# The preparation and the first attention of a two-layer transformer kernel, made one program

## The chip, the cores and the metric

One core of a Trainium2 chip runs the whole kernel as one launch. The time is device microseconds, the median of three runs. TensorE (PE) multiplies and transposes, ScalarE (ACT), VectorE (DVE) and GpSimd (POOL) work on tiles, SyncE (SP) issues the DMAs of this part. Each engine has a list of instructions in a fixed order, and waits on semaphores.

## The reference, cut to what matters

Six blocks follow each other, each added to the states `x` (4 batches of 128 tokens, width 512). The change touches the first alone, a cross attention of 16 heads of 64 over a context of 2048 rows per batch and the 128 states themselves:

```python
xn = layernorm(ctx_1024, ln_x_g, ln_x_b)                  # 4 x 2048 x 512
ln = layernorm(_layernorm(x), ln_l_g, ln_l_b)             # 4 x 128 x 512
q = ln @ Wq                                               # 4 x 128 x 1024
kv = concatenate([xn @ Wkv, ln @ Wkv], axis=1)            # 4 x 2176 x (1024 + 1024)
qn, kn = rmsnorm(q, qn_g) * 64 ** -0.5, rmsnorm(k, kn_g)  # per head of 64
attn = softmax(where(mask, qn @ kn.T, -max))
x = x + (attn @ v) @ Wout + bout
```

## The kernel before

Products that need more than bf16 are made of a high and a low bf16 part of each factor: three products hi x hi, hi x lo, lo x hi.

**`cross0_prepare` (L110 to L449)** is a stage of its own, with a barrier behind it. It loads states and the context of batch 0, normalises both (statistics on VectorE, the root on GpSimd), transposes them on TensorE in 128x128 tiles, splits the context into `x_hi` (ScalarE, L263) and `x_lo` (GpSimd, L229), splits the projection weights `Wkv` in four quads into `w_hi` and `w_lo`, and makes all queries: eight products in float32 (L442), norm, transposes, split, stores of `q_hi` and `q_lo` to DRAM.

**`cross0_attend` (L464 to L1190)** works in 16 units: unit u is batch u // 4, quad of heads u % 4. A unit has 17 steps, one for each 128 rows of keys (16 of context, the last the states). Step n of 272 has on TensorE, in this order:

- `project(n)`: twelve matmuls of 512 columns (L1074 to L1076) that give the keys and values of four heads for 128 rows; it waits for the values' low part of step n - 2
- `turn` (L1085): transposes of normalised keys, due three and four steps after the last projection e of a group of four (the fifth group of a unit is the states alone); `context` (L1093): transposes of the next batch's context. Both go into the one bank KT, and wait until its last user was read
- `values(n - 27)` (L1156 to L1158), `scores(n - 25)` (L1124, L1126), `maximum` (L1106), five to eight steps after e. In the first step of a unit's values they come after the maximum, and wait for `result()` of the unit before.

So LAG = 25 steps of projection run before the first scores. ScalarE copies each projection out (`copies`, L838 to L840), evacuates the turned keys, and does the exponentials. VectorE does in step n, in this order: `result`, `values_low`, `seed(n - 24)` (it writes minus the maximum into the score bank ahead of the scores of the next step, L959), `key_low`, `maximum` (L935), `key_norm` (L907), `key_sum` (L900), then normalising (L924) and statistics (L918, L919) of the next batch's context. GpSimd does in step n `key_root` (L780, L781), `context_root`, the low part of the exponentials (L816), mask blocks (L770) and the low part of the turned context. Tables written out by hand say in which step each of these stands: `key_sum` in step e, `key_root` and `key_norm` in e + 1, `turn` in e + 3 and e + 4. The second group of a unit has e at place 7 of the 17, so its root stands at place 8 and its turns at 10 and 11.

Of the kernel before, what the change touches and what calls it, by code (L numbers as in the profile page):

```python
# [16 lines left out]
B = 4  # L17
# [92 lines left out]
def cross0_prepare(nc, t, X, keep, sb, sem):  # L110
# [4 lines left out]
    x_hi, x_lo = keep["x_hi"], keep["x_lo"]  # L115
    q_hi = sb("c0_qhi", [P, PAIRS, TOK], BF16)
    q_lo = sb("c0_qlo", [P, PAIRS, TOK], BF16)
    L = sb("c0_l", [P, B, D], F32)
    xa = sb("c0_xa", [P, 4, D], F32)
    xb = sb("c0_xb", [P, 4, D], F32)  # L120
    LT = sb("c0_lt", [P, C, TOK], F32)
    lt_hi = sb("c0_lthi", [P, C, TOK], BF16)
    lt_lo = sb("c0_ltlo", [P, C, TOK], BF16)
    wq = sb("c0_wq", [P, C, INNER], F32)
    wst = sb("c0_wst", [P, 2, C, 512], F32)
    q32 = sb("c0_q32", [P, B, INNER], F32)
    sq = sb("c0_sq", [P, 2, 512], F32)
    xf = sb("c0_xf", [P, 2, 512], F32)
    ss = sb("c0_ss", [P, B, H0], F32)
    rn = sb("c0_rn", [P, B, H0], F32)  # L130
    gl = sb("c0_gl", [P, C], F32)
    bl = sb("c0_bl", [P, C], F32)
    gx = sb("c0_gx", [P, C], F32)
    bx = sb("c0_bx", [P, C], F32)
    gq = sb("c0_gq", [P, 1], F32)
    gk = sb("c0_gk", [P, 1], F32)
    gqk = sb("c0_gqk", [P, 1], F32)
    lst = sb("c0_lst", [P, B, 6], F32)
    lmv = sb("c0_lmv", [P, B, 2], F32)
    lsd = sb("c0_lsd", [P, 3, B], F32)  # L140
    st = sb("c0_st", [P, 4, 6], F32)
    mv = sb("c0_mv", [P, 4, 4, 2], F32)
    rstd = sb("c0_rstd", [P, 4, 4], F32)
    power = sb("c0_power", [P, 4], F32)
    x_in, id_in, vec_in, gv_in, wq_in = sem("c0_x_in"), sem("c0_id_in"), sem("c0_vec_in"), sem("c0_gv_in"), sem("c0_wq_in")
    ctx_in, w_in = [sem(f"c0_ctx_in{j}") for j in range(4)], [sem("c0_w_in0"), sem("c0_w_in1")]
    w_hi_done, w_lo_done = sem("c0_w_hi"), [sem("c0_w_lo0"), sem("c0_w_lo1")]
    dve_step, pool_step, consts, power_ready = sem("c0_dve"), sem("c0_pool"), sem("c0_consts"), sem("c0_powr")
    var_ready, sd_ready, l_norm = sem("c0_var"), sem("c0_sd"), sem("c0_l_norm")
    l_tp, lt_done, lt_hi_done, lt_lo_done = sem("c0_l_tp"), sem("c0_lt"), sem("c0_lt_hi"), sem("c0_lt_lo")  # L150
    stat_done, xroot_done, xn_ready = sem("c0_stat"), sem("c0_xroot"), sem("c0_xn_r")
    ln_tp, ln_evac, xhi_done, xlo_done = sem("c0_ln_tp"), sem("c0_ln_ev"), sem("c0_xhi_d"), sem("c0_xlo_d")
    q_mm, q_sq, q_ss = sem("c0_q_mm"), sem("c0_q_sq"), sem("c0_q_ss")
    ms_ready, qsd_ready, qn_done, g_ready = sem("c0_ms"), sem("c0_qsd"), sem("c0_qn"), sem("c0_gr")
    q_tp, q_hi_done, q_lo_done = sem("c0_q_tp"), sem("c0_q_hi"), sem("c0_q_lo")
    lt_out, q_out = sem("c0_lt_out"), sem("c0_q_out")
    QN = INNER // 512
    XT = 4 * C

    def ctx(j):  # L160

        return (X, xa, xb, X)[j]

    def turned_q(b, half):

        return ps[:, 2 + half, :].rearrange("p (r n) -> p r n", n=P)

    with nc.Block() as block:

        @block.sync  # L170
        def _(sp):
            def context(j):
                sp.dma_start(ctx(j)[:], t["ctx"][0, j * 512:(j + 1) * 512, :].rearrange("(i p) d -> p i d", p=P))\
                  .then_inc(ctx_in[j], 16)

            def weights(g):
                wkv = t["L0_xattn_Wkv"].rearrange("(c p) n -> p c n", p=P)
                for half in range(2):
                    sp.dma_start(wst[:, g % 2, :, half * 256:half * 256 + 256],
                                 wkv[:, :, half * INNER + g * 256:half * INNER + g * 256 + 256])\  # L180
                      .then_inc(w_in[g % 2], 16)

            sp.dma_start(L[:], t["x"].rearrange("b p d -> p b d")).then_inc(x_in, 16)
            sp.dma_start(identf[:], t["eye"]).then_inc(id_in, 16)
            for dst, src in ((gl, "L0_xattn_ln_l_g_col"), (bl, "L0_xattn_ln_l_b_col"),
                             (gx, "L0_xattn_ln_x_g_col"), (bx, "L0_xattn_ln_x_b_col")):
                sp.dma_start(dst[:], t[src]).then_inc(vec_in, 16)
            context(0)
            sp.dma_start(wq[:], t["L0_xattn_Wq"].rearrange("(c p) n -> p c n", p=P)).then_inc(wq_in, 16)
            context(1)  # L190
            weights(0)
            for dst, src in ((gq, t["L0_xattn_qn_g"]), (gk, t["L0_xattn_kn_g"])):
                for h in range(2):
                    sp.dma_start(dst[h * DH0:h * DH0 + DH0, :], src.rearrange("(d a) -> d a", a=1))\
                      .then_inc(gv_in, 16)
            context(2)
            weights(1)
            sp.wait_ge(ln_tp, C)
            context(3)
            for g in range(2, QUADS):  # L200
                sp.wait_ge(w_lo_done[g % 2], 1)
                weights(g)
            sp.wait_ge(lt_lo_done, C)
            sp.wait_ge(lt_hi_done, C)
            for b in range(B):
                sp.dma_start(t["lt_hi_d"][b], lt_hi[:, :, b * P:(b + 1) * P]).then_inc(lt_out, 16)
                sp.dma_start(t["lt_lo_d"][b], lt_lo[:, :, b * P:(b + 1) * P]).then_inc(lt_out, 16)
            for b in range(B):
                sp.wait_ge(q_hi_done, 2 * b + 2)
                sp.dma_start(t["q_hi_d"][b], q_hi[:, :, b * P:(b + 1) * P]).then_inc(q_out, 16)  # L210
                sp.wait_ge(q_lo_done, 2 * b + 2)
                sp.dma_start(t["q_lo_d"][b], q_lo[:, :, b * P:(b + 1) * P]).then_inc(q_out, 16)
            sp.wait_ge(lt_out, 2 * B * 16)
            sp.wait_ge(q_out, 2 * B * 16)

        @block.gpsimd
        def _(pool):
            step = Steps(pool, pool_step)

            def root(j):  # L220
                pool.wait_ge(stat_done, j + 1)
                step(pool.tensor_scalar(rstd[:, j, :], mv[:, j, :, 1], 1e-5, None, ALU.add))
                pool.tensor_tensor(rstd[:, j, :], rstd[:, j, :], power[:], ALU.pow).then_inc(xroot_done, 1)

            def low(x):
                j, c = divmod(x, C)
                pool.wait_ge(xhi_done, x + 1)
                cols = slice(j * 512, (j + 1) * 512)
                pool.tensor_tensor(x_lo[:, c, cols], xf[:, x % 2, :], x_hi[:, c, cols], ALU.subtract).then_inc(xlo_done, 1)  # L229

            def weight_low(g):
                pool.wait_ge(w_hi_done, g + 1)
                pool.tensor_tensor(w_lo[:, :, g, :], wst[:, g % 2], w_hi[:, :, g, :], ALU.subtract)\
                    .then_inc(w_lo_done[g % 2], 1)

            pool.memset(power[:], -0.5).then_inc(power_ready, 1)
            pool.wait_ge(power_ready, 1)
            root(0)
            root(1)
            low(0)  # L240
            low(1)
            weight_low(0)
            for k in range(7):
                if k == 2:
                    root(2)
                if k == 4:
                    root(3)
                low(2 * k + 2)
                low(2 * k + 3)
                if k == 5:  # L250
                    weight_low(2)

        @block.scalar
        def _(act):
            def context(x):
                j, c = divmod(x, C)
                act.wait_ge(ln_tp, x + 1)
                if x >= 2:
                    act.wait_ge(xlo_done, x - 1)
                act.activation(xf[:, x % 2, :], ps[:, x % 2, :], ACT.Identity, bias=bx[:, c:c + 1],  # L260
                               scale=gx[:, c:c + 1]).then_inc(ln_evac, 1)
                act.wait_ge(ln_evac, x + 1)
                act.activation(x_hi[:, c, j * 512:(j + 1) * 512], xf[:, x % 2, :], ACT.Copy).then_inc(xhi_done, 1)  # L263

# [19 lines left out]
            for k in range(B * QN):  # L284
                act.wait_ge(q_mm, k + 1)
                if k >= 2:
                    act.wait_ge(q_ss, k - 1)
# [163 lines left out]

# [2661 lines left out]
```

## Time and profile before

| | us |
|---|---|
| median of three runs | 2538.76 (2532.03 to 2540.55) |
| profiled execution | 2541.76 |
| its span, first to last instruction | 2539.8 |
| `cross0_prepare`, to the first projection | 95.8 |
| first projection to the scores' first step | 79.3 |

In the profile PE is TensorE's matmuls, PEld its weight loads; a row of a timeline has the start in us, the duration in us, the engine, the line, the operation, the tiles and how many instructions were merged. A matmul's duration in a row is longer than the distance to the next one, since matmuls are pipelined: distances of starts are what it costs.

### The profile page before, as it was taken

How to read it: one execution, taken by the hardware profiler on the slowest of the kernel's cores; microseconds unless marked ns; L12 is line 12 of the kernel's file. 1: busy time of each engine (PE TensorE's matmuls, PEld its weight loads, DVE VectorE, ACT ScalarE, POOL GpSimd, SP SyncE). 2: the span in 40 equal slices, each digit the busy share in tenths (PEclk: the TensorE clock that was granted, in tenths of full speed). 3: DMA queues.
4: the chain of work that ended last, by engine and by line, in shares of the span. 5: the costliest groups of instructions: out<-in, count | busy, mean ns of one | idle time of the engine just before them, and what ended most of it. 6: DMA issues, size and time to landing. Idle time of an engine off the chain costs nothing. (4 is left out here: it accounts for less than half of the span.)

```text
span 2539.8 us, 57508 instructions
## 1 busy us (share of the span) xinstructions
PE 2312.9 (91%) x21955; PEld 1499.9 (59%) x21955; DVE 1826.2 (72%) x3370; ACT 1557.3 (61%) x2912; POOL 1123.5 (44%) x895
## 2 busy tenths in 40 slices
PE   5799999999999999998888699995799899998795
PEld 3346656666566655666445577772567676776442
DVE  7478877888788867776363699995777777766236
ACT  4347666666666666665234499883377676887313
POOL 4437666666666665554100000004367676656100
PEclk8899999999999999998899799997999999999897
DMA  6223233224222321124321699984533434224002
GB/s 212 52 71 93 84 106 83 75 75 125 82 70 79 107 72 42 42 60 152 113 104 39 219 368 364 365 301 165 163 110 118 127 121 127 88 89 161 30 1 85
DMA packets 256273, 313.56 MB, mean 123 GB/s; under 512 B 71792, under 2 KB 183024, under 8 KB 255104
## 3 DMA queue, kind: packets, MB, share of 16 engines
q1 hardware_dynamic: 252048, 301.76, 37.1%
q10 hardware_dynamic: 3312, 6.03, 0.6%
q8 instruction: 175, 2.87, 0.5%
q0 software_dynamic: 640, 2.10, 0.3%
q14 instruction: 98, 0.80, 0.1%
HBM read 226.23 MB, written 47.91 MB: 108 GB/s over the span
## 5 line engine op out<-in xcount | busy, mean ns | idle before, releaser
L816 POOL TENSOR_TENSOR a_plo<-a_p,a_phi 128x512 bf16<-128x512 f32 x272 | 316.0, 1162 | 358.9 <-ACT a_phi L870 358.1
L1074 PE MATMUL ps<-w,a_xhi 128*128 128x512 bf16 x1088 | 413.9, 380 | 6.0 <-PEq L3010 6.0
L1075 PE MATMUL ps<-w,a_xhi 128*128 128x512 bf16 x1088 | 413.8, 380 | 0.0
L1076 PE MATMUL ps<-w,a_xlo 128*128 128x512 bf16 x1088 | 413.8, 380 | 0.0
L2234 POOL TENSOR_TENSOR a_plo<-a_p,a_phi 128x512 bf16<-128x512 f32 x256 | 306.6, 1198 | 178.8 <-ACT a_phi L2271 169.7
L838 ACT ACTIVATE a_kraw<-ps 128x256 f32<-128x256 f32 x272 | 104.2, 383 | 373.5 <-PE ps L1076 371.8
L2366 DVE CUSTOM_DVE_ANT_0 a_junk<-ps,a_biasrow 128x512 bf16<-128x512 f32 x256 | 176.2, 688 | 117.6 <-PE ps L2506 114.6
L893 DVE TENSOR_TENSOR a_v<-ps,a_v 128x256 bf16<-128x256 f32 x272 | 114.3, 420 | 164.3 <-ACT a_v L840 162.8
L2266 ACT ACTIVATE a_p<-ps,a_mcol 128x512 f32<-128x512 f32 x256 | 174.8, 683 | 87.6 <-PE ps L2524 79.9
L907 DVE SCALAR_TENSOR_TENSOR a_kraw<-a_kraw,a_rn 128x1024 f32<-128x1024 f32 (+1 forms) x80 | 154.2, 1928 | 78.3 <-POOL a_rn L781 78.3
L781 POOL TENSOR_TENSOR a_rn<-a_rn,a_power 128x16 f32<-128x16 f32 (+1 forms) x80 | 204.0, 2550 | 6.6
L866 ACT ACTIVATE a_p<-ps,a_mcol 128x512 f32<-128x512 f32 x256 | 178.8, 699 | 21.7 <-POOL a_plo L816 12.7
L959 DVE CAST ps<-a_less 128x512 f32<-128x512 bf16 x256 | 174.6, 683 | 12.7 <-ACT a_p L866 12.6
L1076 PEld LDWEIGHTS ps<-w,a_xlo 128*128 128x128 bf16 x1088 | 106.6, 98 | 129.1 <-issue 1.3
L1075 PEld LDWEIGHTS ps<-w,a_xhi 128*128 128x128 bf16 x1088 | 106.6, 98 | 124.9 <-issue 1.1
L2489 PE MATMUL ps<-a_whi,c_hi 128*128 128x128 bf16 x1024 | 178.9, 220 | 1.4
L2489 PE MATMUL ps<-a_wlo,c_hi 128*128 128x128 bf16 x1024 | 178.7, 220 | 0.0
L2489 PE MATMUL ps<-a_whi,a_clo 128*128 128x128 bf16 x1024 | 178.6, 220 | 0.0
L870 ACT ACTIVATE a_phi<-a_p 128x512 bf16<-128x512 f32 x272 | 171.3, 630 | 8.7
L935 DVE CUSTOM_DVE_ANT_0 a_junk<-ps,a_mrow 128x512 bf16<-128x512 f32 x256 | 173.9, 679 | 0.0
L1074 PEld LDWEIGHTS ps<-w,a_xhi 128*128 128x128 bf16 x1088 | 106.6, 98 | 105.3 <-issue 7.4
L2271 ACT ACTIVATE a_phi<-a_p 128x512 bf16<-128x512 f32 x256 | 161.2, 630 | 8.1
(461 smaller groups left out, 6890.6 us busy)
## 6 DMA issues: line engine op xcount, KB each, us to landing
e_wst<-in_L_ffn_W SPq DMA_DIRECT2D x46, 2048.0 KB, 10.3
a_ks<-a_khi SPq DMA_DIRECT2D x256, 64.0 KB, 2.0
a_ks<-a_klo SPq DMA_DIRECT2D x256, 64.0 KB, 2.1
a_ct<-in_ctxT SPq DMA_DIRECT2D x16, 1024.0 KB, 6.3
a_ks<-k1h_d SPq DMA_DIRECT2D x128, 128.0 KB, 2.5
xa<-in_ctx SPq DMA_DIRECT2D x8, 1024.0 KB, 5.6
k1h_d<-a_khi SPq DMA_DIRECT2D x64, 128.0 KB, 2.1
k1l_d<-a_klo SPq DMA_DIRECT2D x64, 128.0 KB, 1.7
```

Of the source, the lines that this page charges most:

```text
L781: pool.tensor_tensor(rn[:, key_part(j)], rn[:, key_part(j)], power[:, key_part(j)], ALU.pow)\
L816: pool.tensor_tensor(p_lo[:, m % 3, :], p32[:, m % 2, :], p_hi[:, m % 3, :], ALU.subtract)\
L866: act.activation(p32[:, m % 2, :], ps[:, m % 2, :], ACT.Exp, **bias).then_inc(exp_done, 1)
L935: dve.tensor_tensor_reduce(junk[:], ps[:, bank_m(x), :], mrow[:, j * 512:(j + 1) * 512], 1.0, -3e38, ALU.add, ALU.max, mx[:, h, j:j + 1]). ...
L959: dve.tensor_copy(ps[:, m % 2, :], less[:]).then_inc(seeded, 1)
L1074: pe.matmul(out, x_hi[:, c, tile], w_hi[:, c, g, :], start=(c == 0), stop=False)
L1075: pe.matmul(out, x_hi[:, c, tile], w_lo[:, c, g, :], start=False, stop=False)
L1076: last = pe.matmul(out, x_lo[:, c, tile], w_hi[:, c, g, :], start=False, stop=(c == C - 1))
L2234: pool.tensor_tensor(p_lo[:, m % 3, :], p32[:, m % 2, :], p_hi[:, m % 3, :], ALU.subtract)\
L2266: act.activation(p32[:, m % 2, :], ps[:, m % 2, :], ACT.Exp, bias=mcol[:, u // 4, s:s + 1])\
L2366: dve.tensor_tensor_reduce(junk[:], ps[:, bank_m(x), :], biasrow[:, u // 4 % 2, j * 512:(j + 1) * 512], 1.0, -3e38, ALU.add, ALU.max, mx[: ...
L2489: last = pe.matmul(ps[:, VP, i * P:(i + 1) * P], x[:, b % 2, c, tile], w[:, 1, c, quad], start=(c == 0 and k == 0), stop=(c == C - 1 and k ...
```

## The change

`cross0_prepare` goes away and `cross0` does its work inside the attention's own steps. The first context block is loaded first, normalised, turned and split ahead of the loop; the first projection follows. Blocks 1 to 3, the states, the weights of quads 1 to 3 and the mask are prepared in steps 0 to 18. The queries are no longer made all at once in float32: `query_product` makes those of one unit from high and low parts, twelve matmuls of 256 columns in bank KT, one unit ahead; their norm goes with the last key group of a unit (`size` is 2 instead of 1), so they are squared, rooted, normalised, turned and split as keys are, and go from SBUF into `q_both` and `q_low`. The query weights (512 KB a unit) are loaded and split unit by unit. The second context tile `xn1` is gone, so context blocks are loaded later, and their statistics, normalising and turns stand in other steps.

```diff
-    def query_norm / query_high / query_low ...     (all of cross0_prepare)
...
+    WQ_LOAD, WQ_SPLIT, Q_MADE = (10, 6), (12, 8), (14, 12)
+    def size(u, j):
+        return 4 if j < 4 else 2 if u < UNITS - 1 else 1
...
-                ln_stat[at + ((9, 10, 13, 13) if late else (1, 2, 5, 5))[i]].append((b, j, i))
-                ln_norm[at + ((18, 21, 21, 22) if late else (10, 13, 13, 14))[i]].append((b, j, i))
-                ln_turn[at + ((25, 26, 29, 30) if late else (16, 17, 21, 22))[i]].append((b, j, i))
+            begin = at + ((10, 9, 6, 5)[j] if b == 1 else 5)
+                ln_stat[begin + (2, 3, 3, 4)[i]].append((b, j, i))
+                ln_norm[begin + (5, 5, 6, 6)[i]].append((b, j, i))
+                ln_turn[at + (((17, 21, 22, 25), (16, 17, 21, 22))[j] if b == 1 and j < 2 else (13, 16, 17, 21))[i]]\
+                    .append((b, j, i))
+            ln_load[begin].append((b, j))
...
+    def unit_at(n, place):
+        u, s = divmod(n, NT0)
+        return u if s == place[u > 1] and u < UNITS - 1 else None
...
         def _(sp):
+            head_load(0)
+            sp.dma_start(L, t["x"].rearrange("b p d -> p b d")).then_inc(l_in, 16)
+            ...
+            weights(0)
+            head_load(1)
+            query_weights(0)
...
+                u = unit_at(n, WQ_LOAD)
+                if u is not None:
+                    query_weights(u + 1, n)
                 for u, j, pr in k_turn[n]:
                     stack(u, j, pr)
+                    if j == 4 and u < UNITS - 1:
+                        queries(u + 1, k_hi[:, x, 2 * P:4 * P], k_lo[:, x, 2 * P:4 * P])
...
         def _(pool):
+            def query_weight_low(u):
+                pool.wait_ge(wq_hi_done, u + 1)
+                pool.tensor_tensor(wq_lo[:], wqs if u else wq0, wq_hi[:], ALU.subtract).then_inc(wq_lo_done, 1)
...
             for n in range(LAST):
+                if n < 2:
+                    head_low(4 + 2 * n)
+                    head_low(5 + 2 * n)
+                ...
+                if n in (12, 18):
+                    weight_low(2 if n == 12 else 3)
+                u = unit_at(n, WQ_SPLIT)
+                if u is not None:
+                    query_weight_low(u + 1)
                 for u, j in k_norm[n]:
                     key_root(u, j)
...
         def _(act):
                 if 0 <= n < N:
                     copies(n)
+                if n in (0, 1, 4, 5, 8, 9):
+                    head_context_parts(x)
+                    head_context_parts(x + 1)
+                ...
+                u = unit_at(n, WQ_SPLIT)
+                if u is not None:
+                    query_weight_high(u + 1)
                 for u, j, pr in k_turn[n]:
                     turned(u, j, pr)
                 for b, j, c in ln_turn[n]:
-                    context(b, j, c)
+                    context(n, b, j, c)
+                u = unit_at(n, Q_MADE)
+                if u is not None:
+                    query_copies(u + 1)
...
         def _(dve):
+            head_stat(0)
+            (statistics of the states)
+            head_norm(0)
+            weight_high(0), then w_lo of quad 0
+            head_stat(1), normalising of the states, head_norm(1)
             for n in range(FIRST, LAST):
...
                     values_low(n)
+                if n in (1, 3):
+                    head_stat(2 if n == 1 else 3)
+                if n in (3, 6):
+                    head_norm(2 if n == 3 else 3)
+                if n == 5:
+                    dve.wait_ge(q0_root, 1)
+                    (norm of the first queries)
+                if n in (6, 11, 17):
+                    weight_high({6: 1, 11: 2, 17: 3}[n])
...
         def _(pe):
+            def query_product(u):
+                ...
+                for c in range(C):
+                    pe.matmul(out, hi[:, c, :], wq_hi[:, c, :], start=(c == 0), stop=False)
+                    pe.matmul(out, hi[:, c, :], wq_lo[:, c, :], start=False, stop=False)
+                    last = pe.matmul(out, lo[:, c, :], wq_hi[:, c, :], start=False, stop=(c == C - 1))
+                last.then_inc(q_mm, 1)
+            for x in range(C):
+                head_turn(x)
             for n in range(FIRST, LAST):
                 if 0 <= n < N:
                     project(n)
+                if n == 0:
+                    states_turn()
+                if n in (0, 1, 4, 5, 8, 9):
+                    head_turn(x)
+                    head_turn(x + 1)
+                if n == 3:
+                    query_product(0)
+                if n == 5:
+                    query_turn()
                 (turn, context)
+                u = unit_at(n, Q_MADE)
+                if u is not None:
+                    query_product(u + 1)
...
-                stage(cross0_prepare, X, keep)
-                stage(cross0_attend, X, keep)
+                stage(cross0, X, keep)
```

Lines in brackets and a few short forms stand for code that is told in words above.

## Rows read from the trace of the kernel before

**Rows 1.** Windows: span, busy us of PE, PEld, DVE, ACT, POOL; clock, DMA share, GB/s.

```profile
0.00:95.80 95.80, 52.09 (x176) 30.84 (x177) 64.66 (x108) 38.45 (x62) 38.98 (x32) 0.81 0.50 154
175.10:1180.00 1004.90, 988.25 (x9049) 609.54 (x9047) 792.90 (x1510) 663.54 (x1481) 627.55 (x485) 0.99 0.29 81
```

**Rows 2.** Timeline at the seam of the two stages.

```profile
91.38 0.51 SPq L212 DMA_DIRECT2D q_lo_d<-c_qlo  x1
95.81 0.59 PE L1074 MATMUL ps<-w,a_xhi 128*128 128x512 bf16 x1 [5.97 <-PEq L3010]
```

**Rows 3.** Groups of instructions of the first 95 us: busy us, mean ns, idle before.

```profile
L229 POOL TENSOR_TENSOR a_xlo<-c_xf,a_xhi 128x512 bf16<-128x512 f32 x16 | 23.9, 1511 | 17.7 <-ACT a_xhi L263 17.7
L260 ACT ACTIVATE c_xf<-ps,c_bx,c_gx 128x512 f32<-128x512 f32 x16 | 12.3, 768 | 6.7 <-POOL a_xlo L229 6.2 <-PE ps L413 0.6
```

**Rows 4.** Timeline of the prepare stage.

```profile
6.02 2.47 DVE L358 BATCH_NORM_STATS2 c_lst<-c_l 128x6 f32<-128x512 f32 x4 [5.03 <-DMA c_l<-in_x]
16.15 2.19 ACT L280 ACTIVATE c_lthi<-c_lt 128x512 bf16<-128x512 f32 x4
16.16 1.92 DVE L318 TENSOR_SCALAR xa<-xa,c_mv,c_rstd 128x512 f32<-128x512 f32 x4 [1.72 <-POOL c_rstd L223]
28.41 4.07 POOL L233 TENSOR_TENSOR w<-c_wst,w 128x2048 bf16<-128x2048 f32 x1 [2.87 <-DVE w L324]
34.79 3.13 DVE L327 TENSOR_TENSOR w<-c_wst,w 128x2048 bf16<-128x2048 f32 x1
```

**Rows 5.** Windows of TensorE alone: span, busy us, granted clock, DMA share, GB/s.

```profile
33.00:39.40 6.40, 1.75 (x9) 0.76 0.58 173
39.40:43.00 3.60, 3.54 (x11) 0.50 1.07 319
```

**Rows 6.** Timeline of TensorE, the projection of step 25.

```profile
175.08 0.38 PE L1074 MATMUL ps<-w,a_xhi 128*128 128x512 bf16 x1
```

**Rows 7.** Timeline of GpSimd, place 8 of unit 5.

```profile
451.41 0.25 POOL L780 TENSOR_SCALAR a_rn<-a_ms 128x16 f32<-128x16 f32 x1 [0.23 <-DVE a_ms L900]
451.74 2.93 POOL L781 TENSOR_TENSOR a_rn<-a_rn,a_power 128x16 f32<-128x16 f32 x1
```

**Rows 8.** Timeline of ScalarE, the last of place 8's copies.

```profile
451.99 0.40 ACT L840 ACTIVATE a_v<-ps 128x256 bf16<-128x256 f32 x1
```

**Rows 9.** Timeline of VectorE, places 5 to 10 of unit 5.

```profile
442.27 0.68 DVE L918 BATCH_NORM_STATS2 a_st<-a_xn 128x6 f32<-128x512 f32 x1
...
443.78 0.18 DVE L919 BATCH_NORM_AGGREGATE a_mv<-a_st 128x2 f32<-128x6 f32 x1
...
454.70 2.18 DVE L907 SCALAR_TENSOR_TENSOR a_kraw<-a_kraw,a_rn 128x1024 f32<-128x1024 f32 x1 [0.59 <-POOL a_rn L781]
...
457.14 0.68 DVE L959 CAST ps<-a_less 128x512 f32<-128x512 bf16 x1
...
458.55 0.42 DVE L968 TENSOR_TENSOR a_ao<-ps,a_rs 128x256 f32<-128x256 f32 x1
```

**Rows 10.** Timeline of TensorE, place 10 of unit 5 and the next projection.

```profile
458.40 0.60 PE L1085 MATMUL ps<-identf,a_kraw 128*128 128x128 f32 x4
458.84 0.22 PE L1124 MATMUL ps<-a_qboth,a_ks 128*128 128x128 bf16 x1
...
459.50 0.19 PE L1156 MATMUL ps<-a_v,a_phi 128*128 128x65 bf16 x1
...
459.87 0.38 PE L1074 MATMUL ps<-w,a_xhi 128*128 128x512 bf16 x1
...
462.46 0.60 PE L1085 MATMUL ps<-identf,a_kraw 128*128 128x128 f32 x4
```

**Rows 11.** Timelines of GpSimd, VectorE and TensorE, places 7 to 10 of unit 4.

```profile
382.06 1.93 POOL L770 TENSOR_SCALAR a_mrow<-a_mrow 128x512 bf16<-128x512 uint8 x1
387.37 2.17 DVE L907 SCALAR_TENSOR_TENSOR a_kraw<-a_kraw,a_rn 128x1024 f32<-128x1024 f32 x1 [1.53 <-POOL a_rn L781]
390.14 0.60 PE L1085 MATMUL ps<-identf,a_kraw 128*128 128x128 f32 x4
```

More of the change, by code:

```diff
@@ L126, in cross0_prepare @@
[L126 to L147, printed above, removed]
@@ L600, in cross0_attend @@
             held_by = ("ln", part(*use) + 1)
-    def xn(n):
-        return (X, xn1)[n % 2]
+        if unit_at(n, Q_MADE) is not None:
+            before_q[unit_at(n, Q_MADE) + 1] = held_by
+            held_by = ("query", unit_at(n, Q_MADE) + 2)
     def bank_p(n):
@@ L870, in exponent @@
                 act.activation(p_hi[:, m % 3, :], p32[:, m % 2, :], ACT.Copy).then_inc(phi_done, 1)
-            act.wait_ge(vec_in, 48)
+            act.wait_ge(vec_in, 64)
+            for x in range(C):
+                head_context_parts(x)
+            query_weight_high(0)
             for n in range(FIRST, LAST):
@@ L987, in add_result, with head_stat @@
                 dve.tensor_tensor(X[:, b, :], X[:, b, :], ps[:, bank_o(b), :], ALU.add).then_inc(res_done, 1)
+            def head_stat(j):
+                dve.wait_ge(c_in[j], 16)
+                for i in range(4):
+                    last = dve.bn_stats(st[:, i, :], head_context(j)[:, i, :])
+                step(last)
+                for i in range(4):
+                    last = dve.bn_aggr(hmv[:, j, i, :], st[:, i, :])
+                last.then_inc(c_stat, 1)
+                dve.wait_ge(c_stat, j + 1)
@@ new lines, in head_norm, with weight_high @@
+            def head_norm(j):
+                dve.wait_ge(c_root, j + 1)
+                for i in range(4):
+                    last = dve.tensor_scalar(head_context(j)[:, i, :], head_context(j)[:, i, :], hmv[:, j, i, 0:1],
+                                             hrstd[:, j, i:i + 1], ALU.subtract, ALU.mult)
+                last.then_inc(c_norm, 1)
+            def weight_high(g):
+                dve.wait_ge(w_in[g % 2], 32 * (g // 2 + 1))
+                dve.tensor_copy(w_hi[:, :, g, :], wst[g % 2]).then_inc(w_hi_done, 1)
@@ new lines, in _ @@
+            dve.memset(onesb[:], 1.0).then_inc(consts, 1)
+            head_stat(0)
+            dve.wait_ge(l_in, 16)
+            for b in range(B):
+                last = dve.bn_stats(st[:, b, :], L[:, b, :])
+            step(last)
+            for b in range(B):
+                last = dve.bn_aggr(lmv[:, b, :], st[:, b, :])
+            last.then_inc(l_stat, 1)
+            dve.wait_ge(l_stat, 1)
+            head_norm(0)
+            weight_high(0)
+            dve.wait_ge(w_hi_done, 1)
@@ L1058, in bank_free @@
                 kind, count = held
-                pe.wait_ge(ktlo_done if kind == "turn" else ln_evac, count)
+                pe.wait_ge({"turn": ktlo_done, "ln": ln_evac, "query": q_cp}[kind], count)
             def project(n):
```

672 lines of the change are left out of this document (323 added, 349 removed).

## The prediction

> **What bounds the kernel now.** I read the windows by stage first [rows 1]. Up to 95.8 us no engine is full: TensorE is busy 52 us, VectorE 65. This is the prepare stage. From 175.1 to 1180 us TensorE is busy 988 of 1005 us at full clock, the other engines 62 to 79%: the attention is bound by TensorE, so each microsecond of work or wait that is put on TensorE there is added to the time, and each one taken from the time before it is gained. The seam comes next [rows 2]: the last query store is issued at 91.4, the first projection starts at 95.8. Then the timelines of one step of the steady attention, which show how much room each helper engine leaves ahead of TensorE's next use [rows 7 to 10]; this is where I expect the change to be decided. Call a place in a unit of 17 steps s0 to s16.
>
> **Part 1, the head: gain.** Context block 0 is now the first transfer, and a first transfer of 1 MB is used at 6.02 [rows 4]. Its statistics take 2.9 (2.47 and the aggregates), those of the latents stand before the normalising and take as much, the normalising 1.92 [rows 4]: 13.8. Then four chunks go through ScalarE (0.77, and 0.55 for the high part) and GpSimd (1.5 as the mean of the stage) with two buffers [rows 3, 4], about 8.5: the last low part at 22.4. The first weights' parts on VectorE (3.13 for the low one [rows 4]) are done by then. So the first projection moves from 95.8 to about 22.4: 73.4 earlier.
>
> Not all of it lasts to step 25, where the scores begin (175.08 now [rows 6]). TensorE gets, between projections, 12 chunk transposes of 0.44 [rows 10] (5.3), the latents' 16 (1.8) and the first query product with its turn (1.5), some of it at half clock: about 10. And it waits, because VectorE and GpSimd now do the rest of the preparation inside the steps. I followed each engine's written order with the durations of rows 3, 4 and 7 to 10; the waits that end last are estimates:
> - steps 3 and 4: statistics of blocks 2 and 3 and the normalising of 2 stand ahead of the values' low part: 2.0 and 3.4.
> - step 5: the first query's norm stands on VectorE behind the key norm, which waits on GpSimd behind two low parts and the query's root; TensorE waits at query_turn: 7.4.
> - steps 7 and 8: key_low behind block 3's normalising and weight_high, then the key stacks on the DMA queue behind six query copies: 2.7 and 2.2.
> - step 14: weight_low(2), 4.07 [rows 4], and the split of the next query weights stand on GpSimd ahead of the key root: 5.6, and 4.0 more at the query product, which needs the bank that key_low frees.
> - step 17: the transposes of context (1,0) wait for its normalising: 5.2.
> These are 32.5. Waits like these cost clock too: between 33.0 and 39.4 TensorE was busy 1.75 of 6.4 us, and the next 3.6 us ran at 0.50 [rows 5]; I take 3 us for it. Gain: 73.4 - 10 - 32.5 - 3 = 28. Bounds: 48, if the 7.4, the 9.6 of step 14 and the clock cost nothing; 20, if VectorE and GpSimd hold each other up all through: the low part takes 1.51 as a mean of the stage [rows 3], a quarter of the 4.07 for four times the columns is 1.02 [rows 4].
>
> The Trainium skill (SBUF — State Buffer, section "SBUF: two separate sides") says that GpSimd and a VectorE instruction with two SBUF inputs exclude each other for the whole instruction. The rows agree: 1.51 us where both work, 1.02 where GpSimd works by itself [rows 3, 4]. By that rule the first projection would come up to 3.1 later, at 25.5, and the gain would be 25.
>
> **Part 2, work added on TensorE in the steady part.** Twelve projection matmuls of 512 columns take 2.60 (459.87 to 462.46 [rows 10]); the query product has twelve of 256 columns: 1.30, in units 1 to 15; unit 1's is in part 1, so 14 x 1.3 = 18.2. The last key group of a unit turns four tiles instead of two: 0.22 (half of 0.44 [rows 10]) x 15 = 3.2. Together 21.4, a certain cost, as nothing else on TensorE goes away. That ScalarE (1.1 for the split, 0.8 for two copies, 0.4) and VectorE (about 1) get more per unit costs nothing by its sum, since they are not full; what counts is where it stands in the order.
>
> **Part 3, the split of the query weights at s8.** At s8 (s12 for units 0 and 1) ScalarE does query_weight_high after the step's copies, GpSimd query_weight_low, and in GpSimd's list this stands ahead of key_root. At the same step the root of the second key group is due. Now: key root from 451.41 to 454.68 [rows 7], key norm on VectorE 454.70 to 456.88 [rows 9], turn on TensorE at 458.40 [rows 10]: 1.5 of room. That this room is all there is, is seen where a mask block stood before the same root in the step before: key norm done at 389.54, turn at 390.14 [rows 11]: 0.6 left, so the root was about 0.9 late and TensorE did not wait.
>
> After: copies end at 452.4 [rows 8]; the high part of 128x1024 is half of 2.19 for 128x2048 [rows 4]: 453.5; the low part is half of 4.07: 2.0 to 2.1, to 455.6; the root 3.27, to 458.9; the key norm 2.18, to 461.1. The turn is 2.7 late. Behind the key norm on VectorE are queued, in the ten units with context to normalise, two statistics that the new table puts at s8 (442.27 to 443.96 is such a pair: 1.7 [rows 9]), then the next values' low part and the seed that the scores of s10 need (1.0): 463.8 instead of a free start at 458.84: 5.0 late. Then at s10 the values wait for result(), which stands behind a maximum (0.7), another statistic (0.8) and its own 0.6: 465.95 against 459.50, 6.4 late [rows 9, 10]. The next projection starts 6.4 late; the steps after it find what they need, so it neither grows nor is won back. Without the statistics (units 12 to 14) the same chain gives 3.9. Unit 1, with s12 and a query product at s14 behind key_low: about 8. Sum: 10 x 6.4 + 3 x 3.9 + 8 = 84. Bounds: 38, if only the late turn costs (14 x 2.7); above, 14 more if the low part takes 3.0 instead of 2.05 (twice the 1.51 of rows 3), and the clock, below.
>
> The other moved pieces I cost at nothing: the context load at s5 and the 512 KB of query weights at s6 have more than two steps to land (a first megabyte is used at 6.02 [rows 4], a step is about 4), and stacks that queue behind them would wait inside the stall above; queries now go from SBUF, with as many transfers, five steps ahead of use.
>
> **Sum**, from the profiled execution, 2541.76 (span 2539.8; the three timed runs have a median of 2538.76, 3 less): 2541.8 - 28 + 21.4 + 84 = 2619, in terms of the median 2616.
>
> **Rivals.**
> - *The split is absorbed (faster).* Place: key_root at s8. If high and low part together delay the root by less than 1.5, no turn is late, nothing queues, and 2539 - 28 + 21 = 2532 is left (2512 with the head's upper bound). For it: GpSimd is busy 62% [rows 1]. Against it: the split can't start before the copies end at 452.4 [rows 8], a microsecond after the root starts now [rows 7], and 3.1 us of two instructions don't fit into 1.5. It decides at a delay of 1.5; I work out 4.2. Chance 0.15.
> - *The clock falls in the stalls (slower still).* In 458.4 to 466.3 TensorE would work some 1.5 of 7.9 us; a stretch of that kind (1.75 of 6.4) was followed by 3.6 us at 0.50 [rows 5], which costs half of it, 1.8. With 14 such places: 25 more, 2641. Against it: VectorE, not TensorE, would then be behind for a step, and hides part. The Trainium skill (TensorE: Matmul & The Clock Gate, section "HAM oscillation — how this bites in real kernels") tells of just this pattern, idle gaps that make each burst start at half rate; by it the time would be this rival's. Chance 0.17.
> - *The transfers decide.* 1.5 MB queued at s5 and s6 ahead of the first key stack of a unit makes the maximum at s8 late, and the split's input too, in the three units with a read-back: 3 to 10 us on top, about 2624. For it: TensorE waits for these stacks in program order. Against: such a wait falls into the stall, which is longer. Chance 0.08.
>
> **How the numbers follow.** The forecast as worked out has 0.60, its own range is 2550 (gain 48, stalls 38) to 2640. With the clock and transfer rivals the slower side holds 0.85, less 0.02 for sums of favourable bounds; the absorbed split has 0.15, of which 0.12 is faster by over 0.3% (about what a measurement of this kernel tells from no change) and the rest within it. The range 2530 to 2655 leaves out most of the faster case and the worst of the clock.
>
> **What would show it.** Right: first projection near 22 us, scores near 147; a unit of 17 steps that grows by 5 to 8 us; GpSimd's key root waiting behind query_weight_low; TensorE's waits led by the turn for the key norm and by the scores for the seed. Wrong: TensorE still busy over 97% in the steady part (the split absorbed), or a first projection after 30 us. The weakest points are the head's list of waits and that VectorE's order keeps the statistics behind the key norm.

## The result, and the profile after

The changed kernel takes 2654.85 us (median of four runs, 2650.73 to 2656.74), the kernel before beside it 2537.74: a ratio of 1.046, with a 95% interval of 1.0445 to 1.0474, 117 us slower. The forecast was 2616, 77 slower. The profiled execution has a span of 2654.3.

The head first. Timelines of TensorE in the changed kernel: its first projection, the waits that last longest, and the first projection of the step in which scores begin.

```profile
23.74 0.61 PE L1070 MATMUL ps<-w,a_xhi 128*128 128x512 bf16 x1 [3.49 <-POOL a_xlo L600]
...
62.35 0.69 PE L1194 MATMUL ps<-identf,a_p 128*128 128x128 f32 x2 [8.38 <-DVE a_p L979]
...
104.63 1.12 PE L1082 MATMUL ps<-identf,a_kraw 128*128 128x128 f32 x4 [4.50 <-DVE a_kraw L817]
108.94 0.37 PE L1186 MATMUL ps<-a_wqhi,a_lqhi 128*128 128x256 bf16 x1 [3.19 <-issue]
...
126.02 0.47 PE L1090 MATMUL ps<-identf,xa 128*128 128x128 f32 x1 [4.65 <-DVE xa L839]
...
152.68 0.38 PE L1070 MATMUL ps<-w,a_xhi 128*128 128x512 bf16 x1
```

The first projection has come from 95.8 [rows 2] to 23.7, 72 us earlier; the scores from 175.1 [rows 6] to 152.7, 22.4 earlier. The other 50 us went, on the way, into waits (31.8) and into work that now stands there, some of it at a lower clock.

Then the steady attention: a window of the changed kernel that holds units 1 to 14, from the end of place 7 of unit 1 (columns as in [rows 1]).

```profile
152.00:1240.00 1088.00, 990.95 (x8613) 606.41 (x8751) 761.05 (x1452) 661.91 (x1466) 630.74 (x471) 0.96 0.29 78
```

TensorE was busy 98% here [rows 1], now 91%, and the granted clock is 0.96 in place of 0.99. The table of waits over the same part (waiter, who released it: us in all, times, longest) says where TensorE stands and what is late before it; "issue" is a wait for which the profile names no engine.

```profile
DVE a_kraw L817 <- POOL a_rn L570: 127.1, 70, 4.8
...
POOL a_wqlo L608 <- ACT a_wqhi L722: 38.4, 14, 5.7
...
PEld ps L1103 <- issue: 23.1, 9, 5.0
...
PE ps L1070 <- issue: 19.7, 6, 5.2
PE ps L1082 <- DVE a_kraw L817: 18.5, 10, 2.7
...
PE ps L1153 <- issue: 14.0, 13, 1.7
PE ps L1121 <- DVE ps L874: 13.6, 11, 1.9
```

TensorE waits for the key norm (L1082), for the seed (L1121) and for the result that frees the values' bank (L1153), in 10 to 13 of 14 units each; the key norm waits for the root, and GpSimd sat idle until the query weights' high part came. The largest sum of TensorE's stands before these three: in units 3 to 11 the maximum at place 8 (its weight load, L1103; the wait shows again at the projection behind it, L1070) waits for the key stacks. Timelines of TensorE's weight loads and of its matmuls in unit 7:

```profile
636.96 0.10 PEld L1103 LDWEIGHTS ps<-a_ks,a_qboth 128*128 128x128 bf16 x1 [4.34 <-issue]
...
637.37 0.63 PE L1070 MATMUL ps<-w,a_xhi 128*128 128x512 bf16 x1 [4.57 <-issue]
```

The last stack that it needs was issued at 629.86 and landed 7.04 us later, at 636.90. Units 3 to 11 wait so for 0.7 to 5.0 us, and less at the turn two places on for it: not at all in 3, 7 and 11. One unit shows the order. Timelines of ScalarE, GpSimd, VectorE and TensorE at places 8 to 10 of unit 6, one engine after the other; the counterpart of [rows 7 to 10].

```profile
554.68 0.39 ACT L693 ACTIVATE a_v<-ps 128x256 bf16<-128x256 f32 x1
555.11 1.06 ACT L722 ACTIVATE a_wqhi<-a_xf 128x1024 bf16<-128x1024 f32 x1
...
556.25 2.13 POOL L608 TENSOR_TENSOR a_wqlo<-a_xf,a_wqhi 128x1024 bf16<-128x1024 f32 x1 [2.37 <-ACT a_wqhi L722]
...
558.34 0.25 POOL L569 TENSOR_SCALAR a_rn<-a_ms 128x16 f32<-128x16 f32 x1
558.68 2.93 POOL L570 TENSOR_TENSOR a_rn<-a_rn,a_power 128x16 f32<-128x16 f32 x1
561.57 1.15 POOL L665 TENSOR_TENSOR a_plo<-a_p,a_phi 128x512 bf16<-128x512 f32 x1
...
552.80 1.21 DVE L810 TENSOR_REDUCE a_ms<-a_sq 128x16 f32<-128x1024 f32 x1
...
561.64 2.17 DVE L817 SCALAR_TENSOR_TENSOR a_kraw<-a_kraw,a_rn 128x1024 f32<-128x1024 f32 x1 [4.43 <-POOL a_rn L570]
563.73 0.68 DVE L833 BATCH_NORM_STATS2 a_st<-xa 128x6 f32<-128x512 f32 x1
...
565.64 0.68 DVE L874 CAST ps<-a_less 128x512 f32<-128x512 bf16 x1
...
567.85 0.42 DVE L883 TENSOR_TENSOR a_ao<-ps,a_rs 128x256 f32<-128x256 f32 x1
...
563.86 0.66 PE L1082 MATMUL ps<-identf,a_kraw 128*128 128x128 f32 x4 [1.18 <-DVE a_kraw L817]
566.39 0.23 PE L1121 MATMUL ps<-a_qboth,a_ks 128*128 128x128 bf16 x1 [1.87 <-DVE ps L874]
568.37 0.21 PE L1153 MATMUL ps<-a_v,a_phi 128*128 128x65 bf16 x1 [1.37 <-issue]
```

High part, low part, root, norm, two statistics, values' low part, seed, and with them on TensorE turn, scores and values: each follows the end of the one before it. The key sum was there at 554.0; GpSimd, idle for 2.37 us ahead of 556.25, could have taken the root then, but its list had the low part first. And the windows of TensorE behind it (span, busy us, granted clock, DMA share, GB/s):

```profile
563.00:567.00 4.00, 1.27 (x12) 1.00 0.07 17
567.00:571.00 4.00, 2.63 (x18) 0.53 0.07 18
571.00:575.00 4.00, 4.00 (x26) 0.62 0.23 63
```

TensorE was busy 1.27 of 4 us, and in the next two windows the clock is near its lower level (1.2 instead of 2.4 GHz): the projection at 569.00 takes 5.1 us to the next operation, where it took 2.6 [rows 10]. Counted from the timelines, eleven projections of units 1 to 14 take 3.4 to 4.7 us from their first to their last matmul instead of 2.4, some 20 us together; before, none does. In units 1, 3, 7 and 11 (8 of the 20) the slow projection follows a wait for key stacks, in the other seven the stall of places 8 to 10.

The table is for all kernels below: the start of the matmul that ends place 7 of a unit (L1138 here), and the distance from one to the next in us. u1 is that from place 8 of unit 1, and so on; units 3 and 7 (and 11) have the read-back of the next batch, unit 13 has no context to normalise.

| kernel | first | u1 | u2 | u3 | u6 | u7 | u13 |
|---|---|---|---|---|---|---|---|
| before | 174.6 | 68.6 | 67.2 | 69.7 | 67.2 | 69.7 | 65.5 |
| after | 152.2 | 81.5 | 80.5 | 81.0 | 78.0 | 80.6 | 72.3 |
| root_first | 151.8 | 78.8 | 75.3 | 78.2 | 71.0 | 79.8 | 67.8 |
| double_low | 152.3 | 81.4 | 83.3 | 85.8 | 78.6 | 85.7 | 74.7 |
| warm | 154.1 | 79.3 | 81.6 | 86.1 | 76.0 | 85.0 | 72.3 |
| no_query | 144.9 | 70.4 | 74.8 | 71.5 | 69.2 | 71.2 | 65.5 |
| split_s9 | 151.2 | 79.4 | 75.3 | 77.9 | 71.0 | 77.9 | 67.8 |
| split_s9_back | 154.0 | 79.3 | 75.3 | 75.1 | 71.0 | 75.4 | 67.8 |
| stats_late | 153.3 | 79.4 | 75.3 | 71.2 | 69.0 | 72.8 | 67.9 |
| head_mended | 151.4 | 74.4 | 73.6 | 71.2 | 69.0 | 71.2 | 67.8 |
| norm_alone | 149.7 | 78.7 | 72.3 | 70.7 | 68.8 | 70.7 | 67.0 |
| step4 | 144.5 | 78.5 | 72.3 | 70.7 | 68.8 | 70.7 | 67.0 |
| mended | 141.5 | 74.7 | 69.8 | 70.7 | 68.8 | 70.7 | 67.0 |
| after_norm_alone | 151.5 | 81.3 | 79.8 | 79.7 | 77.0 | 78.5 | 71.3 |

From "first" to place 7 of unit 15 the 14 units take 946.9 us before and 1085.7 after: 138.9 longer. Less 22.4 in the head, that is the 117.

### The profile page after: what moved, and what is told of

Read it like the earlier page. It is cut to its first block and busy times, and to the rows that moved or that the text cites. A ratio compares the mean times of both kernels' runs of the same rounds, so it can differ in the third digit from the quotient of the medians.

```text
span 2654.3 us, 57641 instructions
## 1 busy us (share of the span) xinstructions
PE 2323.6 (88%) x21793; PEld 1514.6 (57%) x22083; DVE 1815.8 (68%) x3357; ACT 1582.0 (60%) x2950; POOL 1170.9 (44%) x916
## 5 line engine op out<-in xcount | busy, mean ns | idle before, releaser
L1070 PE MATMUL ps<-w,a_xhi 128*128 128x512 bf16 x1069 | 417.5, 391 | 36.3 <-issue 20.1
L1071 PE MATMUL ps<-w,a_xhi 128*128 128x512 bf16 x1086 | 423.3, 390 | 3.0 <-DVE a_v L803 2.1
L817 DVE SCALAR_TENSOR_TENSOR a_kraw<-a_kraw,a_rn 128x1024 f32<-128x1024 f32 (+1 forms) x80 | 159.9, 1999 | 153.2 <-POOL a_rn L570 153.2
L570 POOL TENSOR_TENSOR a_rn<-a_rn,a_power 128x16 f32<-128x16 f32 (+1 forms) x80 | 215.8, 2698 | 6.6
L757 ACT ACTIVATE a_phi<-a_p 128x512 bf16<-128x512 f32 x272 | 171.3, 630 | 8.6
L1121 PE MATMUL ps<-a_qboth,a_ks 128*128 128x128 bf16 x1088 | 155.1, 223 | 19.2 <-DVE ps L874 15.8
L1070 PEld LDWEIGHTS ps<-w,a_xhi 128*128 128x128 bf16 x1088 | 109.2, 100 | 109.7 <-issue 13.4
```

The lines of the kernel that those rows point to most:

```text
L570: pool.tensor_tensor(rn[:, k], rn[:, k], power[:, k], ALU.pow).then_inc(kroot_done, 1)
L1070: pe.matmul(out, x_hi[:, c, tile], w_hi[:, c, g, :], start=(c == 0), stop=False)
L1071: pe.matmul(out, x_hi[:, c, tile], w_lo[:, c, g, :], start=False, stop=False)
```

## The experiments

Four single edits of the changed kernel first. **root_first** moves the low part of the query weights behind the key root:

```diff
-                u = unit_at(n, WQ_SPLIT)
-                if u is not None:
-                    query_weight_low(u + 1)
                 for u, j in k_norm[n]:
                     key_root(u, j)
...
                     pool.tensor_tensor(p_lo[:, m % 3, :], ...).then_inc(plo_done, 1)
+                u = unit_at(n, WQ_SPLIT)
+                if u is not None:
+                    query_weight_low(u + 1)
```

> One move: in GpSimd's list the low part of the query weights stands behind the key root and the exponentials' low part of its step. Theory (the split ahead of the key root makes the turn late, and the rest queues behind it): the key root starts right behind its sum again, no turn waits, the clock stays at 1.0; what remains in the ten units with context is about 2 us, as two statistics still stand at place 8. Ten units shrink by about 7 us, units 12 to 14 by 5, unit 1 by 9: about 93 less, 2562 (2550 to 2580). Rival, the transfers ahead of the first key stack: 2640 to 2655, nothing changes for them. Rival, the statistics at place 8 alone: 2600 to 2630.

2597.15 us (two runs), 1.0227 of before (1.0189 to 1.0266): 58 us of the 117 come from this one place in GpSimd's list. The ordinary units fall as expected to 71, units 3, 7 and 11 do not. There, timeline of TensorE at place 8 of unit 7, and the DMA issues of the same 13 us (KB each, us from issue to landing), in the kernel with the root first:

```profile
605.72 0.59 PE L1103 MATMUL ps<-a_ks,a_qboth 128*128 128x512 bf16 x1 [3.52 <-issue]
```

```profile
xa<-in_ctx SPq DMA_DIRECT2D x1, 1024.0 KB, 5.8
a_xhi<-xh_d SPq DMA_DIRECT2D x2, 512.0 KB, 6.4
a_xlo<-xl_d SPq DMA_DIRECT2D x2, 512.0 KB, 7.2
a_xf<-in_L_xattn_Wq SPq DMA_DIRECT2D x1, 512.0 KB, 8.7
a_ks<-a_khi SPq DMA_DIRECT2D x4, 64.0 KB, 6.8
a_ks<-a_klo SPq DMA_DIRECT2D x4, 64.0 KB, 6.2
```

Key stacks of 64 KB, which land after 2.1 us as a rule (median of the page), take 6 to 7 behind 2.5 MB that were issued at places 5 and 6, and the maximum at place 8 waits 3.5 us for them. In the changed kernel this wait is there too (4.3 us in unit 7); there it takes the place of the wait for the turn.

**double_low** computes the low part twice for units 3 to 15, one unit ahead of each, so in units 2 to 14.

```diff
+                if u > 2:
+                    step(pool.tensor_tensor(wq_lo[:], wqs, wq_hi[:], ALU.subtract))
                 pool.tensor_tensor(wq_lo[:], wqs ...
```

> The low part of the query weights is computed twice, one after the other, for units 3 to 15: 2.1 to 2.2 us more on GpSimd ahead of the key root, 13 times. Theory: TensorE's turn is that much later each time, 28 more (25 to 35): 2683. Rival, the transfers decide: GpSimd's 2.1 us hide in the wait for the stacks, under 8 more. If the clock's fall made most of the loss and not the length of the wait: less than 15 more.

2676.62 in one run, 22 more than after. The 14 units take 33.5 more, and the rest of the kernel behind them, which is the same, was 13 shorter in this one execution; so the units say more than the sum. The place is on the path, though each 2.1 us of it brings 0.6 (u6) to 5 (u7).

**warm** fills TensorE's waits at place 10 of units 3 to 11 with matmuls of ones that nothing reads (20 before the turn, 32 before the scores, 22 before the values).

> Added matmuls of 128 columns whose result nobody reads, 20 ahead of the late turn, 32 ahead of the late scores, 22 ahead of the late values, at place 10 of units 3 to 11: about as long as the waits there (1.2, 1.9, 1.4 us). Theory that the clock's fall behind these waits costs 2.6 us a unit: the granted clock stays at 1.0 there and the kernel is about 23 us faster than the changed one, 2632 (2625 to 2642). If the clock costs nothing on the path, because VectorE is behind anyway: 2650 to 2665.

2661.52 in one run: no gain in sum. Windows of TensorE in that kernel, where the changed kernel had 0.53 and 0.62 (unit 6 starts 3.4 us later here):

```profile
567.00:571.00 4.00, 3.68 (x59) 1.00 0.08 20
571.00:575.00 4.00, 4.00 (x48) 1.00 0.07 16
```

The clock stays up and units 5, 6, 8 and 10 get 2.0 to 2.6 us shorter, as the clock's price asks; unit 9, whose projection had not been slow, wins 0.7, unit 4 nothing. Units 3, 7 and 11 got 4 to 5 longer and ate it. The trace has most of that: the wait there is at place 8, ahead of the fillers, so that 4.1 us of them (distances of starts, unit 3) met waits of only 1.7, and the wait for the stacks ended 0.3 to 1.5 us later; the rest is open.

**no_query** leaves the query product, its weights' load and split and its copies out from unit 1 on.

> Left out: making the queries of units 1 to 15 (weight loads, split, products, copies, norm; the query tiles are filled from the key tiles by as many transfers). The head, the single context tile and the new tables stay. Theory: the head's gain of 22 us, 8 more as the first split no longer stands ahead of a key root in step 12, no products, no late root; about 2 us for the statistics in ten units remain: 2528 (2515 to 2542). If the single context tile, the later loads or the new tables are the loss: over 2590.

2536.78 in one run: the time of before. Scores begin 30 us earlier, and units 1 to 11, though they make no queries, are 1.5 to 7.5 us longer each and give all of it back; 12 to 14, which have no context, are as before. So the work on the context that the change moved too (loads, statistics, normalising, turns) costs on its own the 30 us that this head gains.

From here the edits add up. **split_s9** changes constants alone: `WQ_LOAD, WQ_SPLIT, Q_MADE = (10, 7), (12, 9), (14, 12)`, so from unit 2 on the split stands where no root is due.

> Constants alone: from unit 2 on the query weights are loaded at place 7 instead of 6 and split at place 9 instead of 8, where no key root is due; the query product stays at 12. Order theory (what costs is that the split stands ahead of the key root): the ordinary units fall from 77.7 to the 70.5 to 71.0 us that the kernel with the root first showed (67.2 before, 1.5 of query work, 2 of statistics); units 3, 7 and 11 stay at 77 to 80, because read-back and query weights are still ahead of the key stacks; unit 1 stays at 81.5. Together 2600 us (2588 to 2612). Length theory (2 us more on GpSimd and 1 on ScalarE are too much at any place between 8 and 11): ordinary units stay above 75, 2630 or more.

2596.91, 1.0229 (1.0201 to 1.0257): root_first's time within the spread of either. It is the order, not the length of the work.

**split_s9_back** issues the read-back later: `(5, 9, 13, 23)[j]` becomes `(8, 12, 16, 23)[j]`.

> The kernel with the split at place 9, and besides the read-back of the first two context blocks of the next batch (1 MB each) is issued at places 8 and 12 of units 3, 7 and 11 instead of 5 and 9, and that of the third at 16 instead of 13, so that the first key stacks of the unit no longer queue behind it. Transfer theory: units 3, 7 and 11 fall from about 79 to 71 to 73 us, all others stay: 20 us less than the kernel with the split at place 9, about 2580. Rival (the 1 MB context load and the query weights alone hold the stacks up, or these units are slow for their mask blocks): less than 5 us of difference.

2582.03, 1.0164 (1.0137 to 1.0192): 15 less, not 20; units 3, 7 and 11 lose 2.5 to 4 us each, 9 together. The transfers were a cause, and the context's and the query weights' 1.5 MB are left ahead of the stacks.

**stats_late** moves statistics to places 10 and 11:

```diff
-            begin = at + ((10, 9, 6, 5)[j] if b == 1 else 5)
+            begin = at + ((10, 9, 6, 6)[j] if b == 1 else 6)
+            late = b > 1 or j == 3
...
-                ln_stat[begin + (2, 3, 3, 4)[i]].append((b, j, i))
+                ln_stat[begin + ((4, 4, 5, 5) if late else (2, 3, 3, 4))[i]].append((b, j, i))
...
```

The loads, the roots, the normalising and the turns of these blocks move later with them.

> The kernel with split and read-back moved, and besides the statistics of context blocks (from batch 2 on, and the last block of batch 1) stand at places 10 and 11 instead of 7 to 9, their normalising at 13 and 14, their turns at 16, 17, 4 and 5. Theory that VectorE's row of key norm, two statistics, values' low part, seed and maximum at places 8 to 10 costs the last 2 us of a unit: nine units fall from 70.7 to about 68.7, the time of units before and 1.5 of query work: 18 us less, about 2562. Rival (the 2 us are contention or the clock, not the order): the same as without this edit within 5 us, or slower if places 10 to 14 are as full.

2569.22, 1.0119 (1.0091 to 1.0146): 13 less; u6 comes from 71.0 to 69.0 as expected.

**head_mended** moves `query_root` ahead of the low parts of step 4, and `weight_low` and `query_weight_low` (steps 12, 18 and 29, and place 9 of the later units) behind the key root and the exponentials' low part of their step.

> All of the above, and in GpSimd's list the root of the first queries stands ahead of the two low parts of step 4, and the low parts of weights 2 and 3 and of the query weights of steps 12, 18 and 29 stand behind the key root and the exponentials' low part. Order theory for the head: the wait at the first query's turn (8.4) falls to 4 or 5, those of step 14 (4.5 and 3.2) to 1 or 2; the scores' first step comes from 152.7 to 142 to 146, unit 1 falls from 81.5 to 78.8 or less: 10 to 14 us less than the kernel before it in this list, about 2550, against 2538 of the kernel before the change. Rival: VectorE and ScalarE are as full in the head, the wait goes on to the next step, and less than 4 us are won.

2562.89, 1.0109 (1.0071 to 1.0147): 6 less, which the spread of these runs hardly tells from nothing. The waits of the head stayed: 7.8 at the query's turn, 4.6 at step 14. Units 1 and 2 shrank, but unit 1 is long again in the next kernel; what decides there is open. The miss at step 14 has a cause that I had not seen. Timelines of VectorE and GpSimd in that kernel:

```profile
98.72 5.07 DVE L818 SCALAR_TENSOR_TENSOR a_kraw<-a_kraw,a_rn 128x1024 f32<-128x1024 f32 x1 [2.33 <-POOL a_rn L571]
...
98.66 4.06 POOL L605 TENSOR_TENSOR w<-a_ks,w 128x2048 bf16<-128x2048 f32 x1
```

The root came in time, but the key norm then takes 5.07 us, because GpSimd had begun its low part 0.06 us earlier. **norm_alone** makes GpSimd wait for the norm behind each root:

```diff
+                for u, j in k_norm[n]:
+                    pool.wait_ge(kn_ready, 5 * u + j + 1)
                 m = n - LAG
                 if 0 <= m < N:
                     pool.wait_ge(phi_done, m + 1)
```

> The kernel with the head mended, and besides GpSimd waits, behind each key root, for VectorE's key norm, before it goes on to a low part. Exclusion theory (a subtraction on GpSimd and the key norm on VectorE do not run side by side): the key norm of 128x1024 takes 1.2 us instead of 2.17 in the steady part, and that of step 12, which took 5.07 us beside a low part of 4.06, takes 1.2 as well; the wait for it at step 14 (4.56) falls to about 1, the scores' first step comes from 151.4 to about 148, units 12 to 14 lose up to 0.9 us each, the rest little, as TensorE waits for the norm in few places: 4 to 10 us less than the kernel before it, 2553 to 2559. Rival (the norm takes 2.17 by itself, and the 5.07 was a wait for something else): the norm's durations stay, no time is won, or some is lost as the exponentials' low parts come later.

2550.06, 1.0051 (1.003 to 1.0071): 13 less by the medians. The profiled executions are 8 apart, of which head and units 1 to 14 give 4; the rest lies behind them, where nothing was changed. So only 4 of the 13 are shown to be the edit's, at the low end of the 4 to 10 that were expected. The same norm, and the group of norms of 128x1024 from 150 to 1200 us (busy us, mean ns) with it, in the kernel with the norm alone:

```profile
98.77 1.22 DVE L820 SCALAR_TENSOR_TENSOR a_kraw<-a_kraw,a_rn 128x1024 f32<-128x1024 f32 x1 [2.32 <-POOL a_rn L571]
```

```profile
L820 DVE SCALAR_TENSOR_TENSOR a_kraw<-a_kraw,a_rn 128x1024 f32<-128x1024 f32 x59 | 72.3, 1225 | 52.5 <-POOL a_rn L571 51.2
```

5.07 became 1.22, and the 2.17 of nearly every norm (54 of 56 in units 1 to 14 of the changed kernel), [rows 9] too, became 1.22: 0.95 us of it had been GpSimd's low part of the exponentials, which started with it each time (561.57 above). Units 13 and 14 lose the 0.8 that was expected. TensorE's 4.56 for the norm at step 14 is gone, but its wait for the query product behind it grew from 3.18 to 5.65, as the low part of the query weights now comes later. **after_norm_alone** is the same edit on the changed kernel.

> The changed kernel with one edit: GpSimd waits, behind each key root, for VectorE's key norm before it goes on to the exponentials' low part. If the norm of 128x1024 at place 8 stands on the late chain (split, root, norm, statistics, values' low part, seed, scores), its 0.95 us (2.17 against 1.22) comes off each of the 14 units with a split: 8 to 16 us less than 2655, units of 76.8 in place of 77.7. Rival (the low part that is now later makes the values late instead, or another wait ends last): within 4 us of 2655.

2632.35, 1.0377 (1.0362 to 1.0393): 22 less, more than the 8 to 16 of the norm's 0.95 us; most units shrink by 0.6 to 2.1, unit 12 by 3.2. What makes up the rest was not followed.

**step4** takes in step 4 both roots ahead of the two low parts on GpSimd, and normalises the first queries there.

> The kernel with the norm alone, and besides in step 4 GpSimd takes the roots of the first queries and of the first keys ahead of the two low parts of context, and VectorE normalises the first queries there, ahead of the first keys. Order theory: TensorE's wait at the first query's turn, 7.8 us, goes away but for 1 or 2, and the scores' first step comes 5 to 6 us earlier, at about 142: 5 us less, 2548 to 2554. Rival (GpSimd is full in these steps): the low parts are late instead, TensorE waits at the transposes or projections of steps 8 to 12 and less than 2 us are won.

2545.42, 1.0026 (1.001 to 1.0042): 5 less, as expected. The wait at the query's turn is gone; that at the second turn (for key_low) grows from 2.5 to 5.8 us and eats part of it.

**mended** adds two more orders: the query weights' low part ahead of that of weights 2 (both ahead of the exponentials' low part again, behind the norm), and four normalisings of the first three blocks in one step (`(5, 5, 6, 6)` becomes `(5, 5, 5, 5)`).

> The kernel with step 4 mended, and besides the low part of the query weights stands ahead of that of weights 2 in step 12 (both behind the key norm), and the four normalisings of the next batch's first three blocks stand in one step instead of two, ahead of a key norm that waits for its root. Order theory: TensorE's wait at the query product of step 14 falls from 5.7 to about 1.6, that for the context's transposes (4.6 at step 17, 1.5 in unit 1, 2.3 in unit 2) go, with some 2 us of half clock behind them: 12 to 16 us less than the kernel before it, 2529 to 2534, against 2537 of the kernel before the change. Rival (the waits go on to the next producer, weights 2 or the values' low part): less than 5 us won, 2541 or more.

2535.56 against 2537.28, a ratio of 0.9997 (0.9985 to 1.0009): no different from the kernel before. The waits for the context's transposes are gone as expected; at step 14 3.65 us are left (for key_low), and 1.6 appear at step 19. In this kernel the scores begin 33 us earlier than before, and the 14 units take 980.1 us in place of 946.9, 33.2 more.

## Why the prediction was right or wrong

**Direction and mechanism: right.** The size came out only just, and by luck: 2654.85 is the very end of the range 2530 to 2655 and outside the 2550 to 2640 of the working, since two errors of one sign add up (6 less gain, 33 more loss). The split at place 8, ahead of the root, is the largest single loss: 58 of the 117 us come back with its place alone. The chain was named link by link and it is the chain of unit 6. Its length too: the values of place 10 start 17.3 us after the matmul that ends place 7 (568.37 less 551.05), before 11.1 (459.50 [rows 10] less 448.36): 6.2 late, for the 6.4 of part 3. Unit 6 grew by 10.8; 1.5 of query work and 2.5 of half clock (5.1 instead of 2.6) make up most of the rest.

**The step that failed is the sum of part 3: 84 us where 117.5 were measured** (138.9 less the 21.4 of part 2). What it left out was the rival "the clock falls in the stalls", which had a chance of 0.17. Its mechanism is shown: 0.53 and 0.62 behind the stall, 1.00 where warm filled it. Its price was put at 1.8 a unit, and the eleven slow projections add up to 20 us, 1.8 each. The argument against it, that VectorE would be behind for a step and hide part, did not hold: TensorE was busy 4.00 of 4 us at 0.62, and four of the units that warm filled won 2.0 to 2.6 us. The Trainium skill (TensorE: Matmul & The Clock Gate, section "HAM oscillation — how this bites in real kernels") describes this pattern, bursts that start at the lower clock behind an idle gap, and the trace agrees in eleven of fourteen units, where a projection behind a wait runs slowly. The other 13.5 us are spread over the units; units 1 and 2 alone grew by 8.8 more than worked out (26.2 less 3.0 of query work, against 8 and 6.4), some of it slow projections. Counted from the idle times of TensorE's matmuls, the 117.5 are 71 more of waiting in the 22 us behind place 7 (where part 3 has nearly all of its 84), 12 more of waiting elsewhere (4.55 at unit 1's query product, which part 3 has in that unit's 8; 2.43 and 1.46 for the context's transposes in units 2 and 1, which it does not have), and the 20 of slow projections; some 15 stay open.

**"The other moved pieces I cost at nothing": right in size, not in its reason.** In the changed kernel units 3, 7 and 11 are some 3 us longer than ordinary ones, before 2.5: the transfers cost little on top, as was argued. But it is not the stall that covers them. The wait for the stacks comes first, and the late root is covered by it: all waits of places 8 to 10 together are 5.3 to 5.9 us in units 5, 6, 9 and 10, and 6.3 to 7.3 in 3, 4, 7, 8 and 11. So the third rival, which stood at 0.08, was at work in the changed kernel already. Where the late root was taken away, units 3, 7 and 11 were 6 to 9 us longer than ordinary ones, and moving the read-back later won 15. The statistics at place 8 were in part 3's chain and are worth 2.0 us a unit (71.0 to 69.0 in stats_late) for the 2.5 that it has (6.4 less 3.9).

**Part 2: right.** Units 13 and 14 are 1.5 longer in the kernel with the norm alone (67.0 against 65.5), where TensorE has no wait over 0.2 us in them, and part 2 has 1.30 and 0.22 (15 times 0.22 is 3.3, not 3.2, which changes nothing).

**Part 1: mis-sized, 22.4 in place of 28.** The first projection came 1.3 later than worked out. The waits add up to 31.8 (ten of them, four shown above), the list had 32.5. What was too small is the work with its clock: 72.1 less 31.8 less 22.4 leaves 18, in place of 10 and 3. The 1.02 for a GpSimd that "works by itself" was misread: VectorE was busy 4.00 of the 4.10 us from 28.4 to 32.5 in the kernel before, with statistics, sums and the like that read one tile.

**The absorbed split**, the rival on the other side, needed a root that is less than 1.5 us late. It began 4.3 us after the key sum was there (558.34 against 554.01), where before it had waited 0.23 us for the key sum [rows 7]: not absorbed.

## What to carry to other kernels

Before work is put on an engine with idle time, look at what is next in its list and how late that may come; the same two instructions cost 58 us more at place 8 than at place 9. Where TensorE is the bound, price a new wait with what follows it at half clock. And a change that removes a stage pays only what the stage's work does not cost again: here even with seven edits, most of them of order, 33 us of head bought 33 us of longer units, 21 of them by part 2's count the query work.

## What the runs showed of the hardware that was not expected

A subtraction on GpSimd and the key norm on VectorE (two inputs from SBUF) do not run side by side: the norm takes 1.22 us alone, 2.17 beside a low part of 1.15, 5.07 beside one of 4.06, and the profile books the waiting as the norm's busy time: both times the norm ends 1.1 us behind the low part (563.81 against 562.72, 103.79 against 102.72). The Trainium skill (SBUF — State Buffer, section "SBUF: two separate sides") states that exclusion for the whole instruction, and all three rows agree; the prediction had weighed it for the head alone and took the 2.18 for the norm's own price. The kernel before pays it as well (2.18 in [rows 9]); whether it would gain from the same wait was not tried.
